# DLRM tower, opening stage: one-hot rows in steps between products, id rows loaded early, two look-ups placed later

## Chip, cores and metric

The kernel runs on one core of a Trainium2 chip. The metric is device time in microseconds (us), the median of three executions. The engines are TensorE (PE; its weight loads are shown apart as PEld), VectorE (DVE), ScalarE (ACT), GpSimd (POOL) and SyncE (SP), which here only issues transfers.

## What is computed

512 samples have 40 id fields. Each id picks a row of 64 floats from its field's table. All 780 pairs of fields (i < j) are combined by a 64x64 matrix of their own, and a three-layer perceptron follows.

```python
e = jnp.stack([tbl_f[ids[:, f]] for f in range(40)], axis=1)      # 512 x 40 x 64
viW = jnp.einsum('bpd,pde->bpe', e[:, i_idx, :], W)               # 780 pairs, 64 x 64 each
z = jnp.einsum('bpe,bpe->bp', viW, e[:, j_idx, :])
h = jnp.concatenate([z, dense_ctx], axis=1)                       # 780 + 16
h = jnp.maximum(h @ W_top1 + b_top1, 0.0)
h = jnp.maximum(h @ W_top2 + b_top2, 0.0)
y = h @ W_top3
```

## The kernel before

The fields are held two by two in 20 "pairs" `x[:, k, :]`: 128 partitions (two fields of 64 numbers) by 512 samples, fp32. A pair gets there in one of two ways.

- **Turned** (16 pairs: 1, 3, 5, 7, 8, 9 and on). POOL gathers rows of the tables by indirect transfers, eight for a pair (L302), with a small memset between any two (L297). It starts when the list of all ids, `ids_sb`, has landed (L287). PE transposes them (`turn`, L442, 4 matmuls), and ACT copies the result out of PSUM (L315).
- **Looked up** (4 pairs: 0, 2, 4, 6, with tables of 1000 rows). SP loads the two fields' ids, each broadcast over all partitions (`ids_all`, L251), and their tables (`table`, L255). DVE compares the ids with the row numbers and so makes one-hot rows: 16 instructions of 128x512 for a pair (L380), in four steps of 4. PE multiplies them with the tables (`look_up`, L424): 16 matmuls in the code, which the profile counts as 32, in four steps of 8. ACT copies (L315).

`one_hot` has one buffer, so step i of the next pair's rows waits until PE has used step i of this pair's (`one_hot_used`, `turned`; L375, L377). `ids_all` and `table` have two slots, so the loads for the third and fourth look-up wait in SP's queue until the look-up two before is done (L249), and the weight chunks behind them in SP's program order wait as well.

The work itself is 195 units (`UNITS`). Unit s is a product: PE makes `y_ps` (`multiply`, L472, 4 matmuls by the profile's count; five "inner" units have 8, L478), DVE multiplies it with the leaf pair into `prod` (L402). `y_ps` has three slots, so PE's unit s waits for DVE's product s-3 (L460). After each four units, three units behind, PE sums a round over the features into `z_ps` (`sum_round`, L495, 16 matmuls): the round of units 0 to 3 after unit 6, that of units 4 to 7 after unit 10, and so on. The units of leaf pair k begin at `FIRST[k]`: 0, 1, 3, 7, 11, 16, 22, 30 for k = 1 to 8. Unit 6 is inner; its leaf is `x_mix`, which ACT makes (L326). Unit `FIRST[k]` needs `x[k]`.

The order of everything is written out by hand. Every engine runs the steps s = 0 to 194 in its own queue. `EARLY_JOBS` says which look-ups and turns stand ahead of which unit on PE and ACT: before step 0 the look-ups of pairs 0 and 2 and the turn of pair 1; before step 2 the look-up of pair 4 and the turn of pair 3; before step 10 the look-up of pair 6 and the turn of pair 5. Later turns stand three units ahead of their need (`LEAD`): pair 7 at step 19, pair 8 at step 27. All jobs but the first three share one PSUM bank (`t_ps`), so each waits for the ACT copy of the one before. `ROWS_AT` says at which step DVE makes one-hot rows: those of look-ups 0, 1 and 2 (pairs 0, 2, 4) whole before step 0, those of look-up 3 (pair 6) whole before step 3.

The end of the program (last rounds, the layers of the perceptron, the store) is not touched by the change.

Of the kernel before, what the change touches and what calls it, by code (L numbers as in the profile page):

```python
# [7 lines left out]
ALU = mybir.AluOpType  # L8
ACT = mybir.ActivationFunctionType
F32 = mybir.dt.float32  # L10
I32 = mybir.dt.int32

P = 128
B = 512
BT = B // P
F = 40
D = 64
# [22 lines left out]

EARLY_JOBS = {0: [("look", 0), ("look", 2), ("turn", 1)], 2: [("look", 4), ("turn", 3)], 10: [("look", 6), ("turn", 5)]}
EARLY_PAIRS = 7
ROWS_AT = {0: (0, 1, 2), 3: (3,)}
TK_STEP = 2
PARTIAL_PAIRS = 2
PARTIAL_EVERY = 6
# [92 lines left out]
def dlrm_tower(nc, ids, ids_one_hot, row_numbers, small_tables, tables, dense_t, w_units, w1, b1, w2, b2, w3, out):  # L139
    ctx = ExitStack()  # L140
    with ctx:
        def sb(name, shape, dt=F32):
            return ctx.enter_context(nc.sbuf_tensor(name, shape, dt))
# [4 lines left out]
        def sem(name):  # L148
            return ctx.enter_context(nc.semaphore(name))
# [6 lines left out]
        numbers = sb("numbers", [P, TK])  # L156
        ids_all = sb("ids_all", [P, 2, 2, B], I32)
        table = sb("table", [P, 2, 2, TK, D])
        w_sb = sb("w_sb", [P, W_SLOTS, CHUNK * P])
# [15 lines left out]

        partial = [partial_sb[:, m, :] for m in range(M1 - 1)] + [z_sb[:, 0, :]]
        h1_sb = prod[:, 0:M1, :]
        h2_sb = prod[:, M1:M1 + M2, :]
# [16 lines left out]
        w_loaded = [sem(f"w_loaded{s}") for s in range(W_SLOTS)]  # L195
        table_loaded = [sem(f"table_loaded{s}") for s in range(2)]
        looked_loaded = [sem(f"looked_loaded{s}") for s in range(2)]
        numbers_loaded = sem("numbers_loaded")
# [40 lines left out]
        def _(sp):  # L239
            def load_weights(c):  # L240
# [3 lines left out]
                sp.dma_start(w_sb[:, c % W_SLOTS, :], w_units[c]).then_inc(w_loaded[c % W_SLOTS], 16)  # L244

            def load_tables(n):
                if n >= 2:

                    sp.wait_ge(turned, TURN_SEQ["look", LOOKS[n - 2]] + 1)  # L249
                for h in range(2):  # L250
                    sp.dma_start(ids_all[:, n % 2, h, :],  # L251
                                 ids_one_hot[2 * n + h:2 * n + h + 1, :].to_broadcast([P, B])
                                 ).then_inc(looked_loaded[n % 2], 16)
                for h in range(2):
                    sp.dma_start(table[:, n % 2, h, :, :], small_tables[2 * n + h]).then_inc(table_loaded[n % 2], 16)  # L255

            sp.dma_start(ids_sb[:], ids.rearrange("(t p) f -> p t f", p=P)).then_inc(ids_loaded, 16)
            sp.dma_start(numbers[:], row_numbers).then_inc(numbers_loaded, 16)
            load_tables(0)
            load_tables(1)  # L260
            load_weights(0)
            for c in range(1, CHUNKS):
                if c + 1 < len(LOOKS):
                    load_tables(c + 1)
                load_weights(c)
# [94 lines left out]
        def _(dve):  # L360
# [5 lines left out]

            def make_rows(n):
                slot = n % 2
                dve.wait_ge(looked_loaded[slot], 32 * (n // 2 + 1))
                if n == 0:  # L370
                    dve.wait_ge(numbers_loaded, 16)
                for first in range(0, TK, TK_STEP):
                    if n > 0 and first + TK_STEP < TK:

                        dve.wait_ge(one_hot_used, (TK // TK_STEP - 1) * (n - 1) + first // TK_STEP + 1)  # L375
                    elif n > 0:
                        dve.wait_ge(turned, TURN_SEQ["look", LOOKS[n - 1]] + 1)  # L377
                    for k in range(first, first + TK_STEP):
                        for h in range(2):
                            ins = dve.tensor_scalar(one_hot[:, h, k, :], ids_all[:, slot, h, :],  # L380
                                                    numbers[:, k:k + 1], None, ALU.is_equal)
                    ins.then_inc(one_hot_made, 1)

# [20 lines left out]
            for s in range(STEPS):  # L404
                for n in ROWS_AT.get(s, ()):
                    make_rows(n)
                for job in JOBS_AT[s]:
                    if job[0] == "partial" and job[1]:
                        add_partial(job)
                multiply(s)  # L410
# [5 lines left out]
        def _(pe):  # L416
            def look_up(pair, dst):
                n = LOOKS.index(pair)
                pe.wait_ge(table_loaded[n % 2], 32 * (n // 2 + 1))
                for k in range(TK):  # L420
                    if k % TK_STEP == 0:
                        pe.wait_ge(one_hot_made, TK // TK_STEP * n + k // TK_STEP + 1)
                    for h in range(2):
                        ins = pe.matmul(dst[D * h:D * h + D, :], table[:, n % 2, h, k, :], one_hot[:, h, k, :],  # L424
                                        start=(k == 0), stop=(k == TK - 1))
                    if k == TK - 1:
                        ins.then_inc(turned, 1)
                    elif k % TK_STEP == TK_STEP - 1:
                        ins.then_inc(one_hot_used, 1)
# [175 lines left out]
```

## Time and profile before

| | |
|---|---|
| median of 3 executions | 370.56 us |
| lowest, highest | 369.31, 371.61 us |
| profiled execution: time | 369.65 us |
| profiled execution: span, first to last instruction | 367.8 us |
| mean granted TensorE clock | 0.991 |
| PE busy | 347.9 us (95%) |
| DVE busy | 259.8 us (71%) |
| POOL busy | 154.0 us (42%) |
| ACT busy | 38.4 us (10%) |

A share of busy time is a mean over the span. The order of work that the change touches lies in the first 75 us, so the rows further down are mostly of that stretch. Times in a timeline or a chain are from the span's start. A group of matmuls in a timeline begins when the first begins; they are pipelined, so the distance between two groups tells more than the duration of one matmul. "issue" in the chain is time in which the engine waited for nothing that the profile shows.

### The profile page before, as it was taken

To read this page: it belongs to the slowest core of one execution; us is meant where nothing else is said; L and a number is where in the kernel's file an instruction comes from. 1 tells how busy PE (TensorE), PEld (TensorE's weight loads), DVE (VectorE), ACT (ScalarE), POOL (GpSimd) and SP (SyncE) were. 2 spreads that over 40 slices of the span, in tenths; PEclk is the share of its full clock that TensorE was granted. 3 is DMA by queue.
4 is the path that set the end of the run, shared out by engine and by line. 5 is a ranking of instruction groups with operands and counts; after the bars stand their busy time and mean duration, and the time that the engine had idled before them with its cause. 6 is when DMAs were issued, how large, how long until landed. Compare 5 with 4: busy or idle time off the path is not lost.

```text
span 367.8 us, 4723 instructions
## 1 busy us (share of the span) xinstructions
PE 347.9 (95%) x1848; PEld 117.8 (32%) x1848; DVE 259.8 (71%) x271; ACT 38.4 (10%) x61; POOL 154.0 (42%) x261
## 2 busy tenths in 40 slices
PE   0999399999999999999999999999999999999997
PEld 0333122333333333333333333333233333333342
DVE  3974971787787877676768877887768787877430
ACT  1011201030100201010010300000000001200132
POOL 6888888027776755344434544243323100000000
PEclk9999879999999999999999999999999999999999
DMA  7378121102641422112112220122022000000000
GB/s 188 139 222 337 22 81 25 27 37 81 223 135 26 130 76 76 16 65 73 46 32 73 70 59 26 65 70 68 12 65 68 5 0 2 0 0 3 0 1 0
DMA packets 11449, 24.29 MB, mean 66 GB/s; under 512 B 3858, under 2 KB 3858, under 8 KB 11299
## 3 DMA queue, kind: packets, MB, share of 16 engines
q1 hardware_dynamic: 7330, 19.79, 16.2%
q0 software_dynamic: 4096, 4.20, 5.4%
q8 instruction: 14, 0.23, 0.3%
q14 instruction: 9, 0.07, 0.1%
HBM read 23.98 MB, written 0.00 MB: 65 GB/s over the span
## 4 chain that ended last, share of the span: by engine, by line
PE 94%; DVE 3%; DMA 1%; issue 1%; ACT 0%; SPq 0%
PE y_ps L472 47%; PE z_ps L495 25%; PE t_ps L424 6%; PE t_ps L451 4%; PE y_ps L503 3%; PE t_ps L442 2%; DVE one_hot L380 2%; PE y_ps L533 2%; PE y_ps L424 2%; PE y_ps L478 2%; DMA ids_all<-in_ids_one_hot 1%; PE t_ps L539 0%; ACT x L315 0%; DVE prod L402 0%; ACT prod L357 0%
## 5 line engine op out<-in xcount | busy, mean ns | idle before, releaser
L402 DVE TENSOR_TENSOR prod<-y_ps,x 128x1024 f32<-128x1024 f32 x190 | 220.9, 1217 | 74.4 <-PE y_ps L472 74.0
L472 PE MATMUL y_ps<-x,w_sb 64*128 64x512 f32 x760 | 180.9, 607 | 0.8 <-issue 0.7
L302 POOL DMA_INDIRECT rows<-in_tbl,ids_sb x128 | 122.6, 958 | 131.4 <-PE y_ps L472 99.1
L472 PEld LDWEIGHTS y_ps<-x,w_sb 64*128 64x128 f32 x760 | 66.7, 186 | 104.3 <-issue 53.3
L495 PE MATMUL z_ps<-prod,selector 128*32 128x512 f32 x780 | 94.9, 602 | 0.0
L495 PEld LDWEIGHTS z_ps<-prod,selector 128*32 128x32 f32 x780 | 20.5, 110 | 67.9 <-issue 34.4
L380 DVE TENSOR_SCALAR one_hot<-ids_all,numbers 128x512 f32<-128x512 int32 x64 | 27.5, 504 | 7.4 <-DMA ids_all<-in_ids_one_hot 7.4
L424 PE MATMUL t_ps<-one_hot,table 128*64 128x512 f32 x96 | 22.9, 633 | 8.8 <-DVE one_hot L380 8.8
L297 POOL MEMSET spacer<- 128x128 f32 x127 | 30.7, 242 | 0.1
L315 ACT ACTIVATE x<-t_ps 128x512 f32<-128x512 f32 x18 | 10.8, 599 | 191.3 <-PE t_ps L442 145.1
L451 PE MATMUL t_ps<-z_sb,w_sb 128*128 128x512 f32 x32 | 15.9, 618 | 0.0
L424 PEld LDWEIGHTS t_ps<-one_hot,table 128*64 128x64 f32 x96 | 7.2, 145 | 23.4 <-issue 23.4
L478 PE MATMUL y_ps<-x,w_sb 64*64 64x512 f32 x40 | 6.3, 709 | 6.7 <-DVE prod L402 6.7
L326 ACT ACTIVATE x_mix<-x 64x512 f32<-64x512 f32 x20 | 12.6, 628 | 0.5
L331 ACT ACTIVATE z_sb<-z_ps 128x512 f32<-128x512 f32 x6 | 3.6, 597 | 80.6 <-PE z_ps L495 80.6
L442 PE MATMUL t_ps<-ident,rows 128*128 128x128 f32 x60 | 9.8, 286 | 1.4 <-ACT x L315 1.4
L503 PE MATMUL y_ps<-z_sb,w_sb 128*128 128x512 f32 x24 | 10.8, 601 | 0.0
L442 PEld LDWEIGHTS t_ps<-ident,rows 128*128 128x128 f32 x60 | 6.3, 140 | 13.3 <-issue 8.7
L413 DVE TENSOR_TENSOR partial_sb<-y_ps,partial_sb 128x512 f32<-128x512 f32 x3 | 2.1, 692 | 10.0 <-PE y_ps L503 10.0
L451 PEld LDWEIGHTS t_ps<-z_sb,w_sb 128*128 128x128 f32 x32 | 5.4, 189 | 10.2 <-issue 10.2
L424 PE MATMUL y_ps<-one_hot,table 128*64 128x512 f32 x32 | 7.0, 592 | 0.0
L533 PE MATMUL y_ps<-prod,w_sb 128*128 128x512 f32 x16 | 7.0, 592 | 0.0
(30 smaller groups left out, 36.8 us busy)
## 6 DMA issues: line engine op xcount, KB each, us to landing
w_sb<-in_w_units SPq DMA_DIRECT2D x25, 512.0 KB, 3.3
ids_all<-in_ids_one_hot SPq DMA_DIRECT2D x8, 256.0 KB, 4.6
table<-in_small_tables SPq DMA_DIRECT2D x8, 256.0 KB, 5.3
rows<-in_tbl,ids_sb POOLq DMA_INDIRECT x128, 2.5
w_sb<-in_w SPq DMA_DIRECT2D x1, 1792.0 KB, 8.0
w_sb<-in_w SPq DMA_DIRECT2D x1, 512.0 KB, 4.4
ids_sb<-in_ids SPq DMA_DIRECT2D x1, 80.0 KB, 2.2
z_sb<-in_dense_t SPq DMA_DIRECT2D x1, 32.0 KB, 9.5
```

The source lines that it names most:

```text
L297: pool.memset(spacer[:], 0.0).then_inc(spaced, 1)
L302: pool.indirect_dma_start(rows[:, n % ROW_SLOTS, bt, h * D:(h + 1) * D], None, tables[f], bass.IndirectOffsetOnAxis(ap=ids_sb[:, bt, f:f + ...
L380: ins = dve.tensor_scalar(one_hot[:, h, k, :], ids_all[:, slot, h, :], numbers[:, k:k + 1], None, ALU.is_equal)
L402: dve.tensor_tensor(prod[:, at:at + 2, :], y_ps[:, s % Y_SLOTS], leaf, ALU.mult).then_inc(prod_ready, 1)
L424: ins = pe.matmul(dst[D * h:D * h + D, :], table[:, n % 2, h, k, :], one_hot[:, h, k, :], start=(k == 0), stop=(k == TK - 1))
L442: ins = pe.transpose(dst[:, P * bt:P * bt + P], rows[:, at % ROW_SLOTS, bt, :], ident[:])
L451: ins = pe.matmul(dst, w1_sb[:, b, P * m:P * m + P], z_sb[:, b, :], start=(b % 2 == 0), stop=(b % 2 == 1))
L472: ins = pe.matmul(y_ps[:, slot, h, :], w_sb[own, c % W_SLOTS, at:at + P], x[own, m, :], start=True, stop=True)
L478: ins = pe.matmul(y_ps[(low, high)[h ^ bank], slot, bank, :], w_sb[own, c % W_SLOTS, at + D * bank:at + D * bank + D], x[own, 4 * unit[1] ...
L495: ins = pe.matmul(z_ps[q:q + 32, :], selector[:, 30 - row - 2 * n:62 - row - 2 * n], prod[:, 2 * (u % G_UNITS) + n, :], start=(n == 0 and ...
L503: return pe.matmul(h1_ps[m], w1_sb[:, b, P * m:P * m + P], z_sb[:, b, :], start=(b == FIRST_LATE), stop=(b == BANKS - 1))
L533: ins = pe.matmul(h2_ps[m], w2_sb[:, k, P * m:P * m + P], h1_sb[:, k, :], start=(k == 0), stop=(k == M1 - 1))
```

## The change

Four things are done.

1. **SP's order.** The row numbers and the two id rows of look-up 0 are issued first, `ids_sb` behind them. Then the tables of look-up 0, ids and tables of look-up 1, weight chunk 0, and at once, without a wait, ids and tables of look-ups 2 and 3, then the other weight chunks.
2. **Buffers.** `table` has four slots, one for each look-up. `ids_all` is no tile of its own any more: it is the last eight slots of `x` (pairs 12 to 19), which are filled much later.
3. **DVE's order.** One-hot rows are made a step (4 instructions) at a time. All of look-ups 0 and 1 and steps 0 and 1 of look-up 2 before step 0; its steps 2 and 3 before steps 1 and 2; the four steps of look-up 3 before steps 4, 7, 10 and 13.
4. **PE's and ACT's order.** Look-up of pair 4 and turn of pair 3 before step 3 instead of 2; turn of pair 5 before step 11 instead of 10; look-up of pair 6 before step 16 instead of 10.

The counts of compute instructions, matmuls and bytes do not change.

```diff
-EARLY_JOBS = {0: [("look", 0), ("look", 2), ("turn", 1)], 2: [("look", 4), ("turn", 3)], 10: [("look", 6), ("turn", 5)]}
+EARLY_JOBS = {0: [("look", 0), ("look", 2), ("turn", 1)], 3: [("look", 4), ("turn", 3)], 11: [("turn", 5)],
+              16: [("look", 6)]}
 EARLY_PAIRS = 7
-ROWS_AT = {0: (0, 1, 2), 3: (3,)}
+
 TK_STEP = 2
+TK_STEPS = TK // TK_STEP
+ROWS_AT = {0: [(n, i) for n in range(2) for i in range(TK_STEPS)] + [(2, 0), (2, 1)], 1: [(2, 2)], 2: [(2, 3)],
+           4: [(3, 0)], 7: [(3, 1)], 10: [(3, 2)], 13: [(3, 3)]}
...
-        ids_all = sb("ids_all", [P, 2, 2, B], I32)
-        table = sb("table", [P, 2, 2, TK, D])
+        table = sb("table", [P, len(LOOKS), 2, TK, D])
...
+        ids_all = x[:, NP - 2 * len(LOOKS):NP, :].bitcast(I32)
...
+            def load_ids(n):
+                for h in range(2):
+                    sp.dma_start(ids_all[:, 2 * n + h, :], ids_one_hot[2 * n + h:2 * n + h + 1, :].to_broadcast([P, B])
+                                 ).then_inc(looked_loaded[n], 16)
+
             def load_tables(n):
-                if n >= 2:
-
-                    sp.wait_ge(turned, TURN_SEQ["look", LOOKS[n - 2]] + 1)
                 for h in range(2):
-                    sp.dma_start(ids_all[:, n % 2, h, :],
-                                 ids_one_hot[2 * n + h:2 * n + h + 1, :].to_broadcast([P, B])
-                                 ).then_inc(looked_loaded[n % 2], 16)
-                for h in range(2):
-                    sp.dma_start(table[:, n % 2, h, :, :], small_tables[2 * n + h]).then_inc(table_loaded[n % 2], 16)
-
+                    sp.dma_start(table[:, n, h, :, :], small_tables[2 * n + h]).then_inc(table_loaded[n], 16)
+
+            sp.dma_start(numbers[:], row_numbers).then_inc(numbers_loaded, 16)
+            load_ids(0)
             sp.dma_start(ids_sb[:], ids.rearrange("(t p) f -> p t f", p=P)).then_inc(ids_loaded, 16)
-            sp.dma_start(numbers[:], row_numbers).then_inc(numbers_loaded, 16)
             load_tables(0)
+            load_ids(1)
             load_tables(1)
             load_weights(0)
+            for n in range(2, len(LOOKS)):
+                load_ids(n)
+                load_tables(n)
             for c in range(1, CHUNKS):
-                if c + 1 < len(LOOKS):
-                    load_tables(c + 1)
                 load_weights(c)
...
-            def make_rows(n):
-                slot = n % 2
-                dve.wait_ge(looked_loaded[slot], 32 * (n // 2 + 1))
-                if n == 0:
+            def make_rows(n, step):
+                if n == 0 and step == 0:
                     dve.wait_ge(numbers_loaded, 16)
-                for first in range(0, TK, TK_STEP):
-                    if n > 0 and first + TK_STEP < TK:
-
-                        dve.wait_ge(one_hot_used, (TK // TK_STEP - 1) * (n - 1) + first // TK_STEP + 1)
-                    elif n > 0:
-                        dve.wait_ge(turned, TURN_SEQ["look", LOOKS[n - 1]] + 1)
-                    for k in range(first, first + TK_STEP):
-                        for h in range(2):
-                            ins = dve.tensor_scalar(one_hot[:, h, k, :], ids_all[:, slot, h, :],
-                                                    numbers[:, k:k + 1], None, ALU.is_equal)
-                    ins.then_inc(one_hot_made, 1)
+                if step == 0:
+                    dve.wait_ge(looked_loaded[n], 32)
+                if n > 0 and step < TK_STEPS - 1:
+
+                    dve.wait_ge(one_hot_used, (TK_STEPS - 1) * (n - 1) + step + 1)
+                elif n > 0:
+                    dve.wait_ge(turned, TURN_SEQ["look", LOOKS[n - 1]] + 1)
+                for k in range(TK_STEP * step, TK_STEP * step + TK_STEP):
+                    for h in range(2):
+                        ins = dve.tensor_scalar(one_hot[:, h, k, :], ids_all[:, 2 * n + h, :],
+                                                numbers[:, k:k + 1], None, ALU.is_equal)
+                ins.then_inc(one_hot_made, 1)
...
             for s in range(STEPS):
-                for n in ROWS_AT.get(s, ()):
-                    make_rows(n)
+                for n, step in ROWS_AT.get(s, ()):
+                    make_rows(n, step)
```

## Rows read from the trace of the kernel before

**Rows 1.** The page: busy time by engine; granted clock in 40 slices.

```profile
PE 347.9 (95%) x1848; PEld 117.8 (32%) x1848; DVE 259.8 (71%) x271; ACT 38.4 (10%) x61; POOL 154.0 (42%) x261
PEclk9999879999999999999999999999999999999999
```

**Rows 2.** Chain that ended last: start us, us, what; the opening and two full-clock pieces.

```profile
2.25 4.57 DMA ids_all<-in_ids_one_hot
...
8.85 8.74 PE t_ps L424 x32
...
25.04 0.73 issue
...
27.76 7.04 PE t_ps L424 x32
...
36.13 1.08 PE y_ps L472 x4
...
46.50 1.99 PE y_ps L478 x8
48.48 2.50 PE z_ps L495 x16
50.98 2.78 PE y_ps L472 x12
...
70.53 3.63 PE y_ps L472 x16
...
89.23 1.02 PE y_ps L478 x8
...
92.16 1.85 PE z_ps L495 x16
```

**Rows 3.** Waits of PE over the span: us in total, times, longest.

```profile
PE y_ps L478 <- DVE prod L402: 6.7, 1, 6.7
PE t_ps L442 <- ACT x L315: 1.4, 2, 0.7
```

**Rows 4.** Windows: start:end, length, busy of each engine, PEclk, DMA share, GB/s.

```profile
8.00:12.00 4.00, 3.15 (x8) 1.11 (x10) 4.00 (x11) 0.00 (x0) 3.46 (x5) 1.00 1.03 396
...
40.00:42.00 2.00, 0.00 (x0) 0.00 (x0) 2.00 (x6) 0.00 (x0) 1.73 (x3) 1.00 0.08 16
42.00:44.00 2.00, 0.00 (x0) 0.00 (x0) 2.00 (x6) 0.00 (x0) 1.73 (x4) 0.73 0.08 16
...
48.00:49.00 1.00, 1.00 (x8) 0.20 (x8) 1.00 (x2) 0.00 (x0) 0.73 (x3) 0.50 0.00 0
```

**Rows 5.** DVE's timeline: start us, us, instructions, idle before and its releaser.

```profile
22.64 6.96 DVE L380 TENSOR_SCALAR one_hot<-ids_all,numbers 128x512 f32<-128x512 int32 x16 [2.20 <-DMA ids_all<-in_ids_one_hot]
...
37.24 1.23 DVE L402 TENSOR_TENSOR prod<-y_ps,x 128x1024 f32<-128x1024 f32 x1 [5.37 <-PE y_ps L472]
...
66.22 4.62 DVE L402 TENSOR_TENSOR prod<-y_ps,x 128x1024 f32<-128x1024 f32 x4 [1.76 <-PE y_ps L472]
```

**Rows 6.** SP's timeline: issues of transfers.

```profile
0.75 0.44 SPq L257 DMA_DIRECT2D ids_sb<-in_ids  x1
...
1.78 0.90 SPq L251 DMA_DIRECT2D ids_all<-in_ids_one_hot  x2
```

**Rows 7.** POOL's timeline: first, eighth and sixteenth gather.

```profile
3.18 1.10 POOL L302 DMA_INDIRECT rows<-in_tbl,ids_sb  x1 [1.71 <-DMA ids_sb<-in_ids]
...
14.53 1.00 POOL L302 DMA_INDIRECT rows<-in_tbl,ids_sb  x1 [0.27 <-POOL spacer L297]
...
27.47 1.00 POOL L302 DMA_INDIRECT rows<-in_tbl,ids_sb  x1 [0.27 <-POOL spacer L297]
```

**Rows 8.** Issues, us to landing: gathers in 28:32, in 36:45; second table in 3.18:3.4.

```profile
rows<-in_tbl,ids_sb POOLq DMA_INDIRECT x3, 5.6
...
rows<-in_tbl,ids_sb POOLq DMA_INDIRECT x6, 2.4
...
table<-in_small_tables SPq DMA_DIRECT2D x1, 256.0 KB, 5.4
```

More of the change, by code:

```diff
@@ L195, in dlrm_tower @@
         w_loaded = [sem(f"w_loaded{s}") for s in range(W_SLOTS)]
-        table_loaded = [sem(f"table_loaded{s}") for s in range(2)]
-        looked_loaded = [sem(f"looked_loaded{s}") for s in range(2)]
+        table_loaded = [sem(f"table_loaded{n}") for n in range(len(LOOKS))]
+        looked_loaded = [sem(f"looked_loaded{n}") for n in range(len(LOOKS))]
         numbers_loaded = sem("numbers_loaded")
@@ L418, in look_up @@
                 n = LOOKS.index(pair)
-                pe.wait_ge(table_loaded[n % 2], 32 * (n // 2 + 1))
+                pe.wait_ge(table_loaded[n], 32)
                 for k in range(TK):
                     if k % TK_STEP == 0:
-                        pe.wait_ge(one_hot_made, TK // TK_STEP * n + k // TK_STEP + 1)
+                        pe.wait_ge(one_hot_made, TK_STEPS * n + k // TK_STEP + 1)
                     for h in range(2):
-                        ins = pe.matmul(dst[D * h:D * h + D, :], table[:, n % 2, h, k, :], one_hot[:, h, k, :],
+                        ins = pe.matmul(dst[D * h:D * h + D, :], table[:, n, h, k, :], one_hot[:, h, k, :],
                                         start=(k == 0), stop=(k == TK - 1))
```

## Prediction

> **What bounds the kernel now.** I read the page first. PE is busy 95% of the span and DVE 71% [rows 1], so the kernel is bound by PE wherever nothing interrupts it, and a change of order can only win back PE's idle time and time at a lower clock. The row of granted clock is full but for two slices around 40 to 55 us: there something happens. The chain of waits comes next. Nearly all of it is PE, one product or look-up after another, with a hole: before unit 6 (46.50) PE stood for 6.7 us, the longest wait after the start, and it waited for a DVE product [rows 2, 3]. DVE's timeline says why: before unit 3's product it made all 16 one-hot instructions of look-up 3, though PE was not to use them before 53.8. The block of 16 for look-up 2, at 22.64, took 6.96 us [rows 5]; from the start of product 2 at 37.24 such a block and product 3 reach to 46.5. PE's three `y_ps` slots were used up. The windows show the second half of the bill. The clock was still 1.00 in 40 to 42, fell within 42 to 44 (mean 0.73), was 0.50, which is the 1.2 GHz level of TensorE's clock, in 48 to 49, and is full again from the next slice of the page on [rows 1, 4]. So the inner unit took 1.99 us and the round behind it 2.50, where later ones take 1.02 and 1.85 [rows 2]: 0.97 + 0.65 = 1.62 us of low clock. Hole and low clock together are 8.3 us, the most that these edits can find there. The second, smaller item is PE waiting for ACT's copies between two jobs of one bank, 2 x 0.7 us [rows 3].
>
> **Prices.** Product on DVE: 4.62 / 4 = 1.155 us each in a row [rows 5]. One-hot step: 6.96 us for 16 [rows 5], less an overlap of some 0.1 with what follows, / 4 = 1.72. PE: look-up 7.04, four units 3.63 (0.91 each), inner unit 1.02, round 1.85 [rows 2]. Turn 0.6 to 0.66. Turn or look-up, then ACT's copy, then the unit that needs it: 0.73 of standing, as at 25.04 [rows 2]. DVE starts a product 1.1 us after PE starts the unit (36.13 and 37.24 for unit 2) [rows 2, 5].
>
> **Part 1, SP's order.** Look-up 0's ids are issued 0.53 us earlier (1.78 before, 1.25 now) [rows 6]. DVE can then make its first step about 0.5 us earlier, at about 8.2. But the second table was issued near 3.18 and took 5.4 us, so it landed at 8.6 [rows 8], and its place in SP's queue stays as it was. PE's first matmul moves from 8.85 to about 8.65: gain 0.2 (bounds 0 and 0.5).
>
> The ids for look-ups 2 and 3 come early, so DVE's 2.20 us of waiting up to 22.64 [rows 5] goes. On its own this is worth nothing: PE did not wait for those rows, since look-up 2 began at 27.76 with its rows all but made.
>
> `ids_sb` pays. It is issued at about 2.15 instead of 0.75, behind two broadcasts of 256 KB. Nothing in the trace has this order. Lower bound for its landing: as fast as before, when POOL could start 2.4 us after the issue (0.75 to 3.18) [rows 6, 7], so 4.5. The nearest row is the broadcast ahead of it, whose second half landed 4.57 us after its issue [rows 2], now at 6.3; the next two transfers landed within 1.8 us of it (8.6 against 6.8) [rows 2, 8], so I add 0.7 for the 80 KB: 7.0. POOL's first gather moves from 3.18 to about 7.2. The eighth starts 4.0 later than at 14.53 [rows 7], at 18.5, and I take 18.8, as DVE and POOL are busy side by side for all of it now. Parts of 4.5 MB (ids and tables of two look-ups 2 MB, chunks 1 to 5 2.5 MB) that used to wait in SP's queue are now issued at once and keep the transfer engines full until about 25 us, at the some 400 GB/s of 8 to 12 us [rows 4] (7 MB in all at 0.4 MB per us are 18 us, after a slower first 7). Gathers landed after 5.6 us in such a stretch, 2.4 in a quiet one [rows 8]: the eighth lands at 24.4 (21.2 to 24.9). PE wants it for turn 1 at about 24.2. I put 0.3 us of standing there (0 to 1.5). The sixteenth starts near 31.5 (27.47 before) and lands near 34.5; turn 3 wants it at 36.1. The third eight are 4 us later too, and turn 5 is not before 51. POOL is ahead by ten and more from there on. Weight chunk 0 keeps its place, chunk 1 is needed at unit 8: nothing.
>
> The Trainium skill (DMA: Bandwidth & Descriptors, Queues, rings and completion order) says that one issuer's transfers start in ring order, while each transfer engine goes round between the queues by packets. The first half speaks against this change, for `ids_sb`; by the second the gathers, which are in POOL's queue, are only slowed and don't wait for the whole 4.5 MB. The 5.6 against 2.4 us agrees with the second; no row here shows the first for `ids_sb`.
>
> **Part 2, the buffers** cost nothing: `x` slots 12 to 19 are written long after DVE's last one-hot step (near 57 us).
>
> **Parts 3 and 4, both queues step by step.** Look-ups 0 and 1 as before, each 0.2 earlier. DVE has rows (2,0) and (2,1) by about 23.5. Unit 0 starts at 25.6, and units 1 and 2 now follow at once (2.8): PE is at look-up 2 at 28.4. DVE: product 0 from 26.7 to 27.9, step (2,2) to 29.6, product 1 to 30.8, step (2,3) to 32.5. PE takes its third step at 31.9 and its fourth at 33.7: covered by 1.2 us, and if that cover went, each us would be one of PE. Look-up 2 ends at 35.45, copy 0.67, turn 3 0.6, and now unit 3 stands directly behind its turn, so 0.73 of copy is bare (before, unit 2 lay over it). Unit 3 starts at t = 37.45.
>
> From t on PE needs: unit 3 to 6 3.75, round 1.85, units 7 to 9 2.78, in all t + 8.4. DVE: product 3 from t + 1.1, step (3,0), products 4 to 6, step (3,1), product 7. Unit 10 waits for product 7: t + 1.1 + 5 x 1.155 + 2 x 1.72 = t + 10.35. So PE stands 2.0 us before unit 10. This is the price of the new order: what is left of the old hole. (Unit 6 waits for product 3, t + 2.3; unit 9 for product 6, t + 7.45: both in time.) Then unit 10 and round 1 (t + 13.1), turn 5 (t + 13.7), another bare copy 0.73, unit 11 at t + 14.45, units 11 to 14 and round 2 to t + 19.95, unit 15 to t + 20.85. Products 10, 11, 12 are done at t + 15.5, 16.7 and 17.9, step (3,3) at t + 19.6: none is late. Look-up 3 runs to t + 27.9, copy 0.73, unit 16 at t + 28.6, units 16 to 18 end at t + 31.4 = 68.85.
>
> Before, the same point (end of unit 18) was 70.53 + 3.63 = 74.16 [rows 2]. The difference is 5.3 us. With turn 1's 0.3 it is **5.0**. As a ledger of PE: -6.7 hole, -1.6 low clock, -0.2 start, +0.7 copy of turn 3, +2.0 before unit 10, +0.7 copy of turn 5, +0.3 turn 1 is -4.8, the rest being rounding of small gaps; look-up 3 has a copy of 0.7 behind it before and after. Behind unit 18 nothing differs: PE's round and units take 5.48 us per four, DVE's products 4.62, so DVE has no debt left to pass on.
>
> The unknown is the clock. No row shows a stand of 2.0 us. Stands of 0.7 left the clock at 1.00, and in the long one it was still 1.00 over the first 2 us [rows 4]. So I cost it at nothing; at the other end it is the whole 1.6.
>
> **Sum.** Profiled execution 369.65 - 5.0 = 364.65. The median of the three is 0.9 above it: 370.56 - 5.0 = 365.6. I give the middle, 365.1. Run-to-run differences of this kernel are about 1%: less than 1% either way (3.7 us) is "the same".
>
> **Rivals.**
> (a) *The clock falls at the new stand.* Against: 2.0 us is nearer to the unhurt first 2 us of the old hole than to its 6.7. For: three bare stretches lie within 15 us. Then 365.1 + 1.6 = 366.7. Chance 0.12.
> (b) *The gathers are late.* `ids_sb` or the gathers take longer than I gave, and turn 1 stands 1 to 3 us. For: all margins there are thin. Against: only the broadcasts stand ahead of it. About 367.2. Chance 0.16.
> (c) *The DVE is never the one that is late*, since unit 10 finds its product (PE slower than I count, or DVE steps shorter): up to 2.0 better, 363.1. Against: the counts are sums of back-to-back rows. Chance 0.08.
> (d) *The other side: `ids_sb` is served after all that SP issues behind it.* Place: turn 1. If it lands only with the first weight chunk, at about 12.5, the eighth gather starts near 24.1 and lands near 29.7: PE stands 5.5 us instead of 0.3, long enough for the clock to fall (1.6). 365.1 + 5.2 + 1.6 = 371.9. Each us of landing is one of time; from a landing after about 10.5 us on, the clock included, the change loses. Against: transfers in SP's queue landed in the order of issue (ids 6.8, second table 8.6 [rows 2, 8]). Chance 0.03.
> (e) *It does nothing*: the hole only moves to another unit. Against: steps are put where DVE has 5 us of idle time (before unit 3's product, 5.37 [rows 5]); only look-up 3's steps fall into busy stretches. About 369.5. Chance 0.04.
>
> **Numbers.** Forecast 0.57, rivals as given. The range that leaves out no more than 2 in 10 takes in (a), most of (b) and part of (c): 363.0 to 367.9. Faster by over 1% (below 366.8): the forecast, (c), most of (a), a third of (b), 0.76 less some for the thin margin, 0.73. Same 0.24. Slower 0.03.
>
> **What would show it.** The hole before unit 6 gone, PE's row of clock full after the start; a wait of PE (unit 10, L472) for a product of about 2.0 us near 46 to 48; waits for ACT's copies of 0.7 before units 3, 11 and 16; POOL's first gather near 7; end of unit 18 near 69. Wrong if PE waits at turn 1 or turn 3 for gathers by over 1 us, if a slice of the clock below 9 remains near 45 us, or if unit 10 finds its product ready.

## The result, and the profile after

The changed kernel takes 366.78 us against 370.27 (medians of six executions each); the forecast was 365.1, with a range of 363.0 to 367.9. Three executions count as slow, over 1.5% above the fastest of their kernel (381.84 us here, 369.60 of `copies_covered`, 1573.47 of the kernel before in a later series), and are left out of every ratio and every count of executions below. The ratio is 0.989, with a 95% interval of 0.987 to 0.992: 1.1% faster, which is 3.9 us (2.9 to 5.0), where 5.0 us were forecast. The profiled execution took 367.68 us with a span of 365.9, 1.9 us less than the span before. The page first: PE is as busy as before, and the row of clock still has a weak slice, the sixth, where the kernel before had two, the fifth and the sixth.

```profile
span 365.9 us, 4723 instructions
PE 349.1 (95%) x1848; PEld 118.1 (32%) x1848; DVE 259.1 (71%) x271; ACT 38.4 (10%) x61; POOL 153.9 (42%) x261
...
PEclk9999989999999999999999999999999999999999
```

PE's waits (us in total, times, longest) answer to [rows 3]. The 6.7 us before the inner unit are gone. In their place stand 1.7 us before another unit, three copies of 0.78, and one short wait for gathers.

```profile
PE y_ps L477 <- ACT x L321: 2.3, 3, 0.8
PE y_ps L477 <- DVE prod L407: 1.7, 1, 1.7
...
PE t_ps L447 <- ACT x L321: 0.7, 1, 0.7
PE y_ps L447 <- DMA rows<-in_tbl,ids_sb: 0.6, 1, 0.6
```

PE's timeline of the opening (start us, us, instructions, idle before) shows each place: turn 1 at 24.45, turn 3 at 36.40, unit 3 at 37.83, unit 10 at 48.68, round 1 at 50.30, unit 11 at 54.67, unit 16 at 69.09.

```profile
24.45 0.66 PE L447 MATMUL y_ps<-ident,rows 128*128 128x128 f32 x4 [0.56 <-DMA rows<-in_tbl,ids_sb]
...
36.40 0.66 PE L447 MATMUL t_ps<-ident,rows 128*128 128x128 f32 x4 [0.70 <-ACT x L321]
37.83 2.85 PE L477 MATMUL y_ps<-x,w_sb 64*128 64x512 f32 x12 [0.78 <-ACT x L321]
...
48.68 1.70 PE L477 MATMUL y_ps<-x,w_sb 64*128 64x512 f32 x4 [1.74 <-DVE prod L407]
50.30 3.00 PE L500 MATMUL z_ps<-prod,selector 128*32 128x512 f32 x16
...
54.67 3.70 PE L477 MATMUL y_ps<-x,w_sb 64*128 64x512 f32 x16 [0.78 <-ACT x L321]
...
69.09 2.85 PE L477 MATMUL y_ps<-x,w_sb 64*128 64x512 f32 x12 [0.79 <-ACT x L321]
```

Unit 10 took 1.70 us where a unit takes 1.13 at full clock, and round 1 3.00 where one takes 1.92. The windows (as in [rows 4]; the clock is the third number from the end) say why. The clock fell in this execution, just behind the new stand.

```profile
46.00:48.00 2.00, 0.94 (x4) 0.11 (x2) 2.00 (x5) 0.00 (x0) 1.50 (x3) 1.00 0.75 258
48.00:50.00 2.00, 1.32 (x4) 0.30 (x4) 2.00 (x3) 0.00 (x0) 1.73 (x3) 0.78 0.16 31
50.00:52.00 2.00, 2.00 (x10) 0.40 (x12) 2.00 (x4) 0.00 (x0) 1.73 (x4) 0.50 0.08 16
52.00:54.00 2.00, 1.89 (x16) 0.62 (x8) 1.64 (x3) 0.07 (x1) 1.46 (x4) 0.87 0.09 16
```

That is rival (a), in the profiled execution and not in all: the mean granted clock was 0.995 in two of the five executions that count and 1.000 in three. In the kernel before it was 0.991 in every one, 17 of them in the first series below.

The gathers (POOL's timeline: first, eighth, sixteenth) are as late as forecast: 7.10, 19.08 and 31.37, against 7.2, 18.8 and 31.5.

```profile
7.10 1.27 POOL L308 DMA_INDIRECT rows<-in_tbl,ids_sb  x1 [5.63 <-DMA ids_sb<-in_ids]
...
19.08 1.00 POOL L308 DMA_INDIRECT rows<-in_tbl,ids_sb  x1 [0.27 <-POOL spacer L303]
...
31.37 1.03 POOL L308 DMA_INDIRECT rows<-in_tbl,ids_sb  x1 [0.27 <-issue]
```

### The profile page after: what moved, and what is told of

It reads as the page before. It is cut to its first block, busy times and chain, and to the rows that moved or that the text cites. A ratio compares the mean times of both kernels' runs of the same rounds, so it can differ in the third digit from the quotient of the medians.

```text
span 365.9 us, 4723 instructions
## 1 busy us (share of the span) xinstructions
PE 349.1 (95%) x1848; PEld 118.1 (32%) x1848; DVE 259.1 (71%) x271; ACT 38.4 (10%) x61; POOL 153.9 (42%) x261
## 4 chain that ended last, share of the span: by engine, by line
PE 87%; issue 8%; DVE 2%; DMA 1%; ACT 1%; SPq 0%; DVEq 0%
PE y_ps L477 45%; PE z_ps L500 24%; PE t_ps L456 4%; PE y_ps L508 3%; PE t_ps L447 2%; PE t_ps L429 2%; PE y_ps L429 2%; PE y_ps L538 2%; DVE one_hot L385 1%; DMA x<-in_ids_one_hot 1%; PE y_ps L483 1%; DVE prod L407 1%; ACT x L321 1%; PE t_ps L544 0%; ACT prod L363 0%
## 5 line engine op out<-in xcount | busy, mean ns | idle before, releaser
L385 DVE TENSOR_SCALAR one_hot<-x,numbers 128x512 f32<-128x512 int32 x64 | 27.2, 496 | 4.9 <-DMA x<-in_ids_one_hot 4.9
L407 DVE TENSOR_TENSOR prod<-y_ps,x_mix 128x1024 f32<-128x1024 f32 x5 | 6.1, 1217 | 0.9 <-issue 0.9
```

The costliest lines, as they stand in the source:

```text
L385: ins = dve.tensor_scalar(one_hot[:, h, k, :], ids_all[:, 2 * n + h, :], numbers[:, k:k + 1], None, ALU.is_equal)
L407: dve.tensor_tensor(prod[:, at:at + 2, :], y_ps[:, s % Y_SLOTS], leaf, ALU.mult).then_inc(prod_ready, 1)
```

## Experiments

All ratios are to the kernel before, run beside them; a smaller number is faster. The changed kernel has 0.989. Each kernel has one profiled execution, and lines are from that one.

### 1. The order on the engines alone

SP's order, its waits and the two-slot buffers are as before the change; DVE's, PE's and ACT's order is the new one.

```diff
-            sp.dma_start(numbers[:], row_numbers).then_inc(numbers_loaded, 16)
-            load_ids(0)
             sp.dma_start(ids_sb[:], ids.rearrange("(t p) f -> p t f", p=P)).then_inc(ids_loaded, 16)
+            sp.dma_start(numbers[:], row_numbers).then_inc(numbers_loaded, 16)
...
             def load_tables(n):
+                if n >= 2:
+                    sp.wait_ge(turned, TURN_SEQ["look", LOOKS[n - 2]] + 1)
...
+                if c + 1 < len(LOOKS):
+                    load_tables(c + 1)
                 load_weights(c)
```

> The order of DVE, PE and ACT as in the changed kernel (one-hot rows in steps, look-ups and turns moved), but SP's order, its two waits and the two-slot buffers as before the change. Theory 1 (the gain is all in the order on DVE and PE, the early loads cover nothing that was late): look-up 2's ids land at 22.6, its step (2,0) is made by 24.4 and (2,1) by 26.1, before unit 0's product is ready near 27, so PE loses nothing; PE starts at 8.85 instead of 8.37 (+0.5) and turn 1 does not stand for gathers (-0.6). Time as the changed kernel within 0.5 us, 366.3 to 367.3. Rival (the order on DVE only works because all ids are there): DVE waits for ids at 22.6 and at look-up 3, look-up 2 begins with rows missing, 368 or more.

Measured: 367.0 us, ratio 0.990 (0.988 to 0.993). DVE waited for look-up 2's ids, and PE did not notice: look-up 2 began right behind unit 2, without a wait.

```profile
23.72 3.66 DVE L382 TENSOR_SCALAR one_hot<-ids_all,numbers 128x512 f32<-128x512 int32 x8 [3.17 <-DMA ids_all<-in_ids_one_hot]
```

```profile
29.67 7.09 PE L426 MATMUL t_ps<-one_hot,table 128*64 128x512 f32 x32
```

### 2. The loads alone

SP's order and the buffers of the change, with the old order on the engines.

```diff
-EARLY_JOBS = {0: [("look", 0), ("look", 2), ("turn", 1)], 3: [("look", 4), ("turn", 3)], 11: [("turn", 5)],
-              16: [("look", 6)]}
+EARLY_JOBS = {0: [("look", 0), ("look", 2), ("turn", 1)], 2: [("look", 4), ("turn", 3)], 10: [("look", 6), ("turn", 5)]}
...
+ROWS_AT = {0: [(n, i) for n in range(3) for i in range(TK_STEPS)], 3: [(3, i) for i in range(TK_STEPS)]}
```

> SP's order and the buffers of the changed kernel, but the order on DVE, PE and ACT as before the change. Theory 1: the hole of 6.7 us before unit 6 stays, since DVE still makes all of look-up 3's rows before product 3; the clock falls in it; start 0.3 to 0.5 earlier, turn 1 stands 0.6: 370.0 to 370.6. Rival (early ids let DVE run ahead and shorten the hole): product 2 is not the last wait and the hole is 2 us shorter, 368.5 or less.

Measured: 369.79 us, ratio 0.999 (0.997 to 1.000), 0.2 us under theory 1's range. The hole is whole (6.8 us), and the clock fell in every execution.

```profile
PE t_ps L427 <- DMA table<-in_small_tables: 8.2, 1, 8.2
PE y_ps L481 <- DVE prod L405: 6.8, 1, 6.8
```

So the gain is in the order on the engines; the loads and buffers move nothing that can be told from zero. Which part of the order it is, the rows in steps or the later places on PE, these two runs don't tell. The first line is new: look-up 0's ids now come early enough that its second table is what PE waits for.

### 3. The id list first again

```diff
+            sp.dma_start(ids_sb[:], ids.rearrange("(t p) f -> p t f", p=P)).then_inc(ids_loaded, 16)
             sp.dma_start(numbers[:], row_numbers).then_inc(numbers_loaded, 16)
             load_ids(0)
-            sp.dma_start(ids_sb[:], ids.rearrange("(t p) f -> p t f", p=P)).then_inc(ids_loaded, 16)
```

> The changed kernel, but the list of all ids is issued first again, ahead of row numbers and look-up 0's ids. Theory 1: the gathers start at 3.2 instead of 7 or so, PE does not stand 0.56 us for them at turn 1, but DVE's first step and PE's first matmul come 0.35 to 0.5 later: 366.3 to 367.0, the same as the changed kernel. Rival (the late gathers cost more than the one wait shows, by contention behind the early loads): 1 us or more better, 365.6 or less.

Measured: 366.5 us, ratio 0.989 (0.987 to 0.992). No wait at turn 1 is left, and PE's first matmul is at 9.50 instead of 8.37, 1.1 us later where 0.35 to 0.5 was expected. Turn 1 starts 0.4 us later than in the changed kernel (24.86 against 24.45), and the two times can't be told apart.

### 4. Rows made while PE does a look-up

```diff
-           4: [(3, 0)], 7: [(3, 1)], 10: [(3, 2)], 13: [(3, 3)]}
+           3: [(3, 0), (3, 1), (3, 2)], 13: [(3, 3)]}
```

> The changed kernel, but steps 0 to 2 of look-up 3's rows stand before product 3 (DVE idle for 5.7 us there while PE runs look-up 2) instead of before products 4, 7 and 10; step 3 stays before product 13. Theory 1 (what is left of the hole is DVE's two steps between products 3 and 7, and the low clock after it): product 3 is not delayed by more than 0.1, PE's stand of 1.7 us before unit 10 goes wholly, and with it the clock's fall of 1.9 us that only some executions show: 1.7 + about 1 on the mean, 363.7 to 364.5, granted clock 1.000 in every execution. Rival (the stand is there for another reason, such as a slow first product after DVE's idle time, or rows made this early wait for PE): 365.5 or more.

Measured: 363.1 us, ratio 0.980 (0.978 to 0.982), clock 1.000 in all five executions. That is 0.6 us better than theory 1's range. PE's list of waits has no DVE product in it any more. DVE's 12 instructions end at 40.01, as product 3 becomes due; it starts 1.25 us after its unit, and the inner unit 6 follows units 3 to 5 without a stand.

```profile
34.81 5.20 DVE L385 TENSOR_SCALAR one_hot<-x,numbers 128x512 f32<-128x512 int32 x12
39.93 3.47 DVE L407 TENSOR_TENSOR prod<-y_ps,x 128x1024 f32<-128x1024 f32 x3
```

```profile
38.68 2.85 PE L477 MATMUL y_ps<-x,w_sb 64*128 64x512 f32 x12 [0.78 <-ACT x L321]
41.45 1.09 PE L483 MATMUL y_ps<-x,w_sb 64*64 64x512 f32 x8
```

### 5. The stand made longer

```diff
-           4: [(3, 0)], 7: [(3, 1)], 10: [(3, 2)], 13: [(3, 3)]}
+           4: [(3, 0)], 7: [(3, 1), (3, 2)], 13: [(3, 3)]}
```

> The changed kernel, but step (3,2) stands before product 7 (with step (3,1)) instead of before product 10. Theory 1 (the length of PE's stand before unit 10 decides whether the clock falls): the stand grows from 1.7 to 3.4 us, and the clock falls in nearly every execution instead of in one of four: mean granted clock 0.991 to 0.996 in most, 1.7 + 1.4 us over the changed kernel, 369.3 to 370.3. Rival (the clock's fall in the profiled execution was chance, unrelated to the stand): the clock is 1.000 in most executions, and only the stand is paid, 368.0 to 368.8.

Measured: 369.09 us, ratio 0.997 (0.995 to 0.998). That is between the two ranges, 0.2 us under the first; the clock decides for theory 1, as it was below 1.000 in nine of ten executions. The stand was 3.30 us. Moving one step takes back two thirds of the gain.

```profile
51.12 1.49 PE L477 MATMUL y_ps<-x,w_sb 64*128 64x512 f32 x4 [3.30 <-DVE prod L407]
52.55 3.20 PE L500 MATMUL z_ps<-prod,selector 128*32 128x512 f32 x16
```

### 6 to 8. Copies covered: both ends, the later end, the first end

`copies_covered` has all three jobs a unit earlier; `later_copies_covered` has turn 5 and look-up 3 earlier, `first_copy_covered` look-up 2 and turn 3. One thing is in neither half: step (3,3), which `copies_covered` has before product 12, stands before product 13 in both. `copies_covered` against experiment 4:

```diff
-EARLY_JOBS = {0: [...], 3: [("look", 4), ("turn", 3)], 11: [("turn", 5)], 16: [("look", 6)]}
+EARLY_JOBS = {0: [...], 2: [("look", 4), ("turn", 3)], 10: [("turn", 5)], 15: [("look", 6)]}
...
-           3: [(3, 0), (3, 1), (3, 2)], 13: [(3, 3)]}
+           2: [(2, 3), (3, 0), (3, 1), (3, 2)], 12: [(3, 3)]}
```

> rows_in_look_up with three jobs a unit earlier, so that a unit which does not need the copy lies over it: look-up 2 and turn 3 before unit 2 (instead of 3), turn 5 before unit 10 (11), look-up 3 before unit 15 (16). Steps (3,0) to (3,2) stand before product 2, (3,3) before product 12. Theory 1 (the three bare copies of 0.78 us cost what they show): against rows_in_look_up 2.3 us less, of which products 2 and 3 late by 0.2 to 0.4 give some back: 360.7 to 361.4. Rival (PE then stands for gathers at turn 3, 1 us earlier than now, or for DVE, which has as much to do in less time): 362 or more.

> rows_in_look_up with turn 5 before unit 10 instead of 11 and look-up 3 before unit 15 instead of 16; look-up 2 and turn 3 stay before unit 3. Theory 1 (each covered copy gives its 0.78 us; what made copies_covered slow belongs to its look-up 2 before unit 2): 361.4 to 362.0, no wait of PE over 1 us. Theory 2 (the pauses in which PE's signals for units 11 and 15 came up to 3.7 us late come with these later jobs): a stand of 1 to 4 us near unit 14 or 18 in some executions, median 363.5 or more, executions apart by over 3 us.

> rows_in_look_up with look-up 2 and turn 3 before unit 2 instead of 3 and steps (3,0) to (3,2) before product 2; turn 5 and look-up 3 stay before units 11 and 16. Theory 1 (the copy's 0.78 is given, less 0.3 for products 2 and 3 that are late): 362.4 to 363.0. Theory 2 (late signals belong to this early part): a stand over 1 us near unit 14 or 18 in some executions, median 363.5 or more, executions apart by over 3 us.

Measured: both ends 366.04 us, ratio 0.988 (0.982 to 0.993), executions from 363.6 to 369.0. The later end alone 361.84, ratio 0.977 (0.975 to 0.979), all five within 0.9 us. The first end alone 363.73, ratio 0.982 (0.980 to 0.984), within 0.3 us.

The later end is a hit by its number, 1.3 us under experiment 4. By its reason it is only half of one. The two copies are covered (1.6 us), but turn 5 now had to wait 1.00 us for its late gathers and turn 1 another 0.21. From the end of look-up 0 to the end of unit 18, the profiled executions take 49.6 us against 50.0 in experiment 4; the rest of their difference is look-up 0 itself, 8.60 us here and 10.10 there, which is told at the end.

```profile
47.05 0.63 PE L447 MATMUL t_ps<-ident,rows 128*128 128x128 f32 x4 [1.00 <-DMA rows<-in_tbl,ids_sb]
...
63.03 3.70 PE L477 MATMUL y_ps<-x,w_sb 64*128 64x512 f32 x16
```

The first end gave nothing: look-up 2 had to wait 0.16 us for its last step, units 2 to 5 took 4.07 instead of 3.70 as product 2 was late, and turn 5's copy was bare for 1.25 instead of 0.78.

Both together, with step (3,3) a product earlier, brought something that neither has alone. In the profiled execution PE stood 2.03 us before unit 14, waiting for product 11, and DVE had not been busy: it began product 11 at 53.23, though PE's unit 11 had started at 49.63. Step (3,3) stands behind product 11 in DVE's order, so DVE did not make it late by working on that step; that its new place matters in some other way is not excluded.

```profile
49.63 2.85 PE L477 MATMUL y_ps<-x,w_sb 64*128 64x512 f32 x12
54.51 1.13 PE L477 MATMUL y_ps<-x,w_sb 64*128 64x512 f32 x4 [2.03 <-issue]
```

```profile
53.23 1.23 DVE L407 TENSOR_TENSOR prod<-y_ps,x 128x1024 f32<-128x1024 f32 x1 [3.48 <-PE y_ps L477]
```

### 9. The last look-up where it was

```diff
-EARLY_JOBS = {0: [...], 3: [("look", 4), ("turn", 3)], 11: [("turn", 5)], 16: [("look", 6)]}
+EARLY_JOBS = {0: [...], 3: [("look", 4), ("turn", 3)], 10: [("look", 6), ("turn", 5)]}
...
-           3: [(3, 0), (3, 1), (3, 2)], 13: [(3, 3)]}
+           3: [(3, 0), (3, 1), (3, 2)], 4: [(3, 3)]}
```

> rows_in_look_up, but look-up 3 and turn 5 stand before unit 10 as before the change, and step (3,3) before product 4 so that its rows are there. Theory 1 (placing look-up 3 later is worth nothing by itself once its rows are made in time; a look-up is 7.04 us of PE wherever it stands): one bare copy of 0.7 instead of two of 0.78, and one more step in front of product 4 with PE late by up to 0.5: 362.2 to 363.3. Rival (the later place matters, as DVE needs the time between): over 364.5.

Measured: 368.0 us, ratio 0.992 (0.989 to 0.994). By the bare number that is the rival's (over 364.5), but not by its reason. The look-up itself went as in theory 1: PE took it at 45.98 with rows ready. The loss is a stand of 1.33 us before unit 14 and one of 3.05 before unit 18, with the clock falling behind it, and once more DVE had nothing to do before its product. This trace has the best view of it, the timeline of all engines from 63 to 71 us:

```profile
64.34 2.85 PE L477 MATMUL y_ps<-x,w_sb 64*128 64x512 f32 x12
...
68.89 0.33 SPq L249 DMA_DIRECT2D w_sb<-in_w_units  x1
68.97 2.36 DVE L407 TENSOR_TENSOR prod<-y_ps,x 128x1024 f32<-128x1024 f32 x2 [3.92 <-remote]
...
70.25 1.22 PE L477 MATMUL y_ps<-x,w_sb 64*128 64x512 f32 x2 [3.05 <-DVE prod L407]
```

Units 15 to 17 started from 64.34 on, one each 0.9 us. DVE's product 15 and SP's load of chunk 7 both wait for `y_ready` to reach 16, the signal of unit 15. In the changed kernel unit 15 started at 60.16 and SP issued at 61.33, 1.2 us later; here it was 4.55. Two engines that have nothing else in common went on within 0.1 us of each other. So the signal came 3.4 us late, or the matmuls ended that much later than their starts tell; it was not DVE. What holds it, and why only in some orders and some executions, stays open, and with it whether the later place of look-up 3 is worth anything by itself.

### 10 to 12. PE busy before the first look-up

28 small matmuls of the identity by itself on PE ahead of the first look-up, on top of `copies_covered`; then 20 on top of experiment 4; then those with the id list first. They compute nothing that is used.

```diff
             pe.wait_ge(ident_ready, 1)
+            for _ in range(28):
+                pe.matmul(y_ps[:, 0, 0, 0:P], ident[:], ident[:], start=True, stop=True)
             for s in range(STEPS):
```

> copies_covered with 28 small matmuls (128 columns, the identity by itself, into a bank that is overwritten later, no output changes) on PE before the first look-up, while PE waits for rows. Theory 1 (the first look-up's 8.6 to 10.1 us instead of 7.04 is TensorE's clock at its lower level after idling, in a stretch of 3.1 to 6.1 us that differs between executions): the stretch falls into the wait, look-up 0 takes 7.1 to 7.6 us, the time is 1.5 to 2.5 us below copies_covered and its executions differ less, 358.5 to 359.8. Rival (the first look-up is slow for another reason, such as its transfers still landing beside it or DVE's pace): look-up 0 as long as before, time as copies_covered.

> rows_in_look_up with 20 small matmuls (128 columns, the identity by itself, overwritten later) on PE before the first look-up. copies_covered_warm showed look-up 0 at full speed (7.09 us by the timeline) but its 28 matmuls ended 2 us too late; 20 should end near 8. Theory 1 (the late gathers are hidden only as long as PE is slow in front of them): look-ups 0 and 1 end at about 22.5 instead of 24 to 25, but the eighth gather still lands at 24.5, so PE now stands some 2 us before turn 1 and most of the 1.6 to 3 us is lost: 361.8 to 363.0. Rival (look-ups are then limited by DVE's steps, so nothing arrives earlier): 363 or more and no stand at turn 1.

> warm_gathers_late with the list of all ids issued first. Theory 1 (with PE fast in the opening, the place of that list in SP's queue decides): no stand at turn 1, unit 0 starts near 24.3 although the first look-up starts 0.4 to 0.8 later: about 0.8 us less than warm_gathers_late, 360.8 to 362.2. Rival (the later ids cost as much as the earlier gathers give): within 0.3 us of warm_gathers_late.

Measured: 366.63 us, ratio 0.989 (0.987 to 0.992); 365.44, ratio 0.986 (0.982 to 0.989); 361.68, ratio 0.977 (0.975 to 0.979). The first was expected to win and did not. Its small matmuls ended at 10.5, so look-up 0 started 2.2 us later than in `copies_covered`, as much as it was shorter: look-up 1 starts at 17.36 in both. And the late signals came again, with 3.74 us before unit 16. There another engine shows them, by another semaphore: look-up 3 took PE from 55.17 to 62.25, unit 15 started at 62.18, and ACT, idle, began the copy of the look-up at 66.31, where in `later_copies_covered` it begins 0.1 us after unit 15's start (63.15 and 63.03).

```profile
55.17 7.09 PE L429 MATMUL t_ps<-one_hot,table 128*64 128x512 f32 x32
62.18 1.13 PE L477 MATMUL y_ps<-x,w_sb 64*128 64x512 f32 x4
67.05 4.43 PE L477 MATMUL y_ps<-x,w_sb 64*128 64x512 f32 x12 [3.74 <-issue]
```

```profile
66.31 0.60 ACT L321 ACTIVATE x<-t_ps 128x512 f32<-128x512 f32 x1 [18.58 <-remote]
```

But its look-up 0 took 7.09 us, and that is what it was for.

The other two are the pair that tells the place of `ids_sb` apart. In `warm_gathers_late` PE is at turn 1 near 22.3 and stands 2.81 us for the gathers. The clock falls (0.50 in the window from 28 to 30), and units 0 to 2 take 4.54 us instead of 2.85.

```profile
25.14 0.66 PE L447 MATMUL y_ps<-ident,rows 128*128 128x128 f32 x4 [2.81 <-DMA rows<-in_tbl,ids_sb]
26.53 4.54 PE L477 MATMUL y_ps<-x,w_sb 64*128 64x512 f32 x12 [0.73 <-issue]
```

With the list first both are gone, in the same places:

```profile
22.84 0.66 PE L447 MATMUL y_ps<-ident,rows 128*128 128x128 f32 x4
24.23 2.85 PE L477 MATMUL y_ps<-x,w_sb 64*128 64x512 f32 x12 [0.73 <-issue]
```

`warm_gathers_late` missed both of its ranges: it has the stand of theory 1, but its time is 2.4 us over that range. The gap of 3.8 us between the two medians, where I expected 0.8, has two parts. In the two executions of `warm_gathers_late` in which the clock stayed at 1.000 the time was 363.6, 2.0 us over `warm_list_first`: that is the stand, 2.81 us where I had put 2, less a first look-up that starts 0.58 earlier (2.2 us by the two profiles). The other 1.8 us is the clock, which I had left out. `warm_list_first` and `later_copies_covered` are the fastest kernels of the study, 2.3% under the kernel before and some 1.3% under the changed one. The two together were not run.

## Why the prediction was right, and where it was off

**The hole and its low clock.** The hole went, as forecast; its low clock with it in three of five executions (see the clock below). Experiment 2 shows that both stay when only the loads change; experiment 1 that the hole goes when only the order changes.

**The loads.** "On its own this is worth nothing" holds for the early ids: ratio 0.999 alone. The cost side was nearly right. `ids_sb` took 4.7 us to land, the eighth gather was 0.3 us later than forecast, and PE stood 0.56 us at turn 1 where I had put 0.3. The start was better, 0.48 instead of 0.2. The sum of the two was forecast at +0.1 and came to +0.1; that two errors of 0.3 cancel is luck. One sentence was wrong without harm: turn 5 is "not before 51" only while PE stands before unit 10. In `later_copies_covered` it came at 46 and waited 1.00 us.

**The new stand.** The mechanism is right. Forecast 2.0 us before unit 10, for product 7: measured 1.74 there, and 0.46 more inside units 7 to 9 (3.31 us instead of 2.85). (The prediction's t + 10.35, with t the start of unit 3, is t + 10.3 by its own terms.) Unit 10 came at t + 10.85, and the difference is one start: product 3 began 1.65 us after its unit instead of 1.1. In experiments 1 and 3 it was 1.64 as well. The cause of this half us isn't known. Experiment 4 takes two of DVE's steps away from this place, and the stand goes; experiment 5 adds one, and it grows to 3.30. Product 3 in the changed kernel:

```profile
39.48 1.22 DVE L407 TENSOR_TENSOR prod<-y_ps,x 128x1024 f32<-128x1024 f32 x1 [5.68 <-PE y_ps L477]
```

**A wrong reading.** Rival (e) was argued away with "steps are put where DVE has 5 us of idle time (before unit 3's product, 5.37 [rows 5])". The 5.37 us stand before product 2, at 37.24, and the change puts no step into them: DVE is idle for 5.68 us before product 3 in the changed kernel too. The price of look-up 3's steps was in the sum all the same, so the forecast did not suffer. But that idle time was the better place, as experiment 4 shows.

**The bare copies.** Forecast 0.73 each before units 3 and 11: measured 0.78.

**The clock.** This is the term that was mis-sized: "I cost it at nothing; at the other end it is the whole 1.6." In the profiled execution it was the other end, about 1.7 us (unit 10: 0.6, round 1: 1.1), and a slice below 9 near 45 us was one of the prediction's own signs of being wrong. On the mean it is neither: whether the clock falls differs between executions of one kernel, and more of them have it the longer the stand. Here are the eleven kernels whose signals come on time, with the longest profiled stand in front and, as "fallen", a mean granted clock below 1.000: none over 1.3 us, fallen in 0 of 20 executions; 1.7 us, in 4 of 17; 2.8 us, in 4 of 6; 3.3 us, in 9 of 10; 6.7 us, in all. The three kernels with late signals (experiments 6, 9 and 10) have stands that need not be the same in every execution: fallen in 1 of 5, 4 of 6 and 5 of 6. So an estimate of the mean price here is 4/17 x 1.7 = 0.4 us.

**The sum.** The end of unit 18, at 68.85 + 0.3 in the forecast, was 71.94 in the profiled execution, 2.8 later: 1.7 of clock, 0.5 of product 3, some 0.3 before unit 3 and in the copies, the rest in gaps too small to name. From there to the end of the span both kernels take the same within 0.3 us (293.6 and 294.0), as forecast. Over all executions the gap is smaller, 5.0 against 3.9 with an interval of 2.9 to 5.0, as three of five keep the clock. The prediction's line for "faster by over 1%" was 366.8, and the median is 366.78: on which side of it the kernel falls is chance. The number that I subtracted from has a scatter of its own: the profiled execution before is 0.9 us under its median, and its first look-up was one of the shorter ones (8.74 us), which is told below.

## What to carry to other kernels

Work that an engine does ahead of need belongs into the time in which that engine waits for the one that bounds the kernel. Here DVE had 5.7 idle us beside a look-up; the change spread the rows over products instead, where PE stood for two of the four steps, and moving three steps into that time (experiment 4) gave nearly as much again as the whole change. A stand of PE can cost more than its length: one of 1.7 us did in 4 of 17 executions, one of 3.3 us in 9 of 10. Before covering a copy, look at what its unit will wait for next: of 1.6 us of copies covered in `later_copies_covered`, later waits for gathers took back most. And early loads have a queue: what is put behind them should be what is needed last, which only shows once the time in front of it shrinks.

## What was not expected of the hardware

**A slow first look-up that the row of clock does not show.** Look-up 0 has the same 32 matmuls as the others, which take 7.05 to 7.09 us. It took 8.74 before the change, 8.65 after, and 8.56 to 10.10 over the eleven kernels in which PE idles before it, and 7.09 in all three in which PE was kept busy. Its first matmuls have a mean of 1,070 ns, its last 592. Other matmuls of 512 columns had 1,084 and 1,061 ns behind the old hole, where the granted clock was 0.50, its lower level (1.2 GHz), and 592 at 2.4 GHz; but here the granted clock reads 1.00 throughout. In `rows_in_look_up` DVE's next step even waited 0.57 us for PE, so DVE did not cause it, and full transfer queues did not either, as they were as full beside the three fast ones. What removes it is shown, PE at work before; that it is the clock is inferred from the two durations. The stretch ended 3.1 to 6.1 us after the first matmul, and with it the profiles of different kernels differ by 1.5 us before anything else does: for single profiles, compare times from the end of look-up 0 on, not from 0. This has a limit. The eighth gather lands when it lands, so a slow look-up 0 hides the wait at turn 1: the changed kernel (look-up 0: 8.65) has 0.56 us of it, `rows_in_look_up` (10.10) none. By that measure the profiled executions take, from there to the end of unit 18, 56.6 us before the change, 54.9 after it, 52.6 and 52.9 in experiments 1 and 3 (no fall of the clock) and 50.0 in experiment 4.

```profile
8.40 10.10 PE L429 MATMUL t_ps<-one_hot,table 128*64 128x512 f32 x32 [8.40 <-DMA table<-in_small_tables]
18.31 7.05 PE L429 MATMUL y_ps<-one_hot,table 128*64 128x512 f32 x32
```

```profile
8.96 7.09 PE L429 MATMUL t_ps<-one_hot,table 128*64 128x512 f32 x32 [0.77 <-DVE one_hot L385]
15.85 7.07 PE L429 MATMUL y_ps<-one_hot,table 128*64 128x512 f32 x32
```

(The first two lines are `rows_in_look_up`'s, the others `warm_list_first`'s.)

**Signals of PE up to 4 us late.** In the profiles of `copies_covered`, `copies_covered_warm` and `look_up_at_10`, the signals of units 11 or 15 or of look-up 3 came 0.4 to 4 us late, to DVE, to SP and to ACT. In the openings of the others the latest are the half us of unit 3 and of turn 5 (1.25 us of bare copy in `first_copy_covered`, 1.12 in `warm_gathers_late`). Little but arrangement differs between these kernels, and the two halves of one of them have no signal over half a us late. The cause is open. `copies_covered` and `look_up_at_10` came out some 5 us over their forecasts with it, so an order that looks best on paper has to be measured in several executions.
